# Graph-attention kernel: from the third head on, ScalarE copies the first of three value parts into packed rows of 132 bytes

## What is computed

```
feats = einsum('bnf,hfu->bhnu', X, W)
dense = e_self[..., :, None] + e_neigh[..., None, :]
dense = leaky_relu(dense, 0.2) + NEG_BIG * (1.0 - A)
att   = softmax(dense, axis=-1)
out   = einsum('bhij,bhju->bhiu', att, feats) + b
x     = layernorm(x + relu(out))
```

## Time and profile before

| what | value |
|---|---|
| median of 3 runs | 3373.38 us (3371.62 to 3376.89) |
| the profiled execution, its own time | 3371.02 us |
| its span, first to last instruction | 3369.2 us |
| PE busy | 3291.4 us, 98% |
| DVE busy | 2387.5 us, 71% |
| ACT busy | 1864.4 us, 55% |
| granted TensorE clock, mean | 0.995 of full |

### The profile page before, as it was taken

The page is one execution under the profiler, slowest core; times in us unless marked ns, Lnnn a source line. Parts: engine busy times, 40 slices in busy tenths (PEclk is TensorE's granted clock), DMA queues, the critical chain, the costliest instruction groups (busy, mean ns, idle before and its releaser), DMA issues.

```text
span 3369.2 us, 125185 instructions
## 1 busy us (share of the span) xinstructions
PE 3291.4 (98%) x57408; PEld 2804.7 (83%) x57408; DVE 2387.5 (71%) x4236; ACT 1864.4 (55%) x2456; POOL 283.6 (8%) x251
## 2 busy tenths in 40 slices
PE   5999999999999999999999999999999999999998
PEld 4978879798896978979789797887979879797896
DVE  4857758587685867858578585785858768586685
ACT  2746547365564645646466473654746547465563
POOL 0020100202001020010201002010020200202001
PEclk8999999999999999999999999999999999999999
DMA  6114141241412315132141421514124141231400
GB/s 189 62 51 135 45 125 54 69 123 40 132 60 83 102 34 141 65 85 94 39 139 54 101 78 43 142 47 123 56 64 127 41 132 60 73 112 34 126 29 25
DMA packets 233486, 280.95 MB, mean 83 GB/s; under 512 B 149888, under 2 KB 149888, under 8 KB 232960
## 3 DMA queue, kind: packets, MB, share of 16 engines
q1 hardware_dynamic: 232960, 272.95, 27.1%
HBM read 205.26 MB, written 34.08 MB: 71 GB/s over the span
## 4 chain that ended last, share of the span: by engine, by line
PE 85%; DVE 7%; DMA 5%; ACT 1%; issue 1%; SPq 0%; DVEq 0%; POOL 0%; ACTq 0%
PE six L856 72%; PE pair L856 10%; DVE mask L695 2%; DMA s_bc<-self_scores 2%; PE six L991 2%; DMA out_dram<-mask 1%; DMA self_scores<-sc_row 1%; PE pair L885 1%; DVE rest L603 1%; PE six L885 1%; DVE x_parts L599 1%; DVE feat L637 1%; ACT step L465 1%; DVE trl L632 0%; ACT trh L430 0%
## 5 line engine op out<-in xcount | busy, mean ns | idle before, releaser
L856 PE MATMUL six<-x_parts,mask 128*128 128x65 bf16 x16384 | 1547.0, 192 | 17.2 <-DVE mask L695 16.6
L856 PEld LDWEIGHTS six<-x_parts,mask 128*128 128x128 fp8e4 x16384 | 1536.2, 97 | 26.0 <-issue 16.0
L856 PE MATMUL six<-rest,mask 128*128 128x65 bf16 x16384 | 1547.1, 195 | 1.5 <-issue 1.2
L856 PE MATMUL six<-third,mask 128*128 128x65 bf16 x16384 | 1546.8, 192 | 0.8 <-issue 0.6
L856 PEld LDWEIGHTS six<-third,mask 128*128 128x128 fp8e4 x16384 | 1536.4, 98 | 1.3 <-issue 1.2
L856 PEld LDWEIGHTS six<-rest,mask 128*128 128x128 fp8e4 x16384 | 1531.0, 96 | 2.5 <-issue 1.8
L465 ACT ACTIVATE step<-s_bc,n_step 128x1024 uint16<-128x1024 f32 x1024 | 1089.4, 1137 | 372.4 <-DVE mask L695 342.9
L695 DVE TENSOR_TENSOR mask<-adj_t,step 128x1024 uint16<-128x1024 uint16 x1024 | 649.9, 685 | 55.9 <-ACT step L465 55.8
L856 PE MATMUL six<-adj_t,x_parts 128*128 128x512 fp8e4 x1536 | 388.4, 380 | 9.1 <-issue 4.9
L408 POOL TENSOR_TENSOR s_bc<-feat,rden 128x512 f32<-128x512 f32 x112 | 124.6, 1117 | 2811.3 <-DVE s_bc L738 2797.6
L856 PEld LDWEIGHTS six<-adj_t,x_parts 128*128 128x128 f16 x1536 | 146.3, 98 | 186.1 <-issue 15.9
(11 more groups left out here) (127 smaller groups left out, 4839.9 us busy)
## 6 DMA issues: line engine op xcount, KB each, us to landing
s_bc<-self_scores SPq DMA_DIRECT2D x128, 512.0 KB, 3.8
mask<-in_adj_dram SPq DMA_DIRECT2D x64, 512.0 KB, 4.0
xs<-in_x_dram SPq DMA_DIRECT2D x128, 256.0 KB, 3.6
adj_nat<-in_adj_dram SPq DMA_DIRECT2D x64, 512.0 KB, 3.5
out_dram<-mask SPq DMA_DIRECT2D x128, 256.0 KB, 3.3
adj_nat<-in_x_dram SPq DMA_DIRECT2D x64, 256.0 KB, 5.7
step<-in_x_dram SPq DMA_DIRECT2D x64, 256.0 KB, 3.8
xs<-in_L_gnn_W_dram SPq DMA_DIRECT2D x1, 2048.0 KB, 11.4
```

The lines of the kernel that those rows point to most:

```text
L856: return pe.matmul(o, l, r, start=start, stop=stop, skip_group_check=True)
```

## The change

A new tile `packed` holds the first part of a head as bf16, elements 2 bytes apart, in rows of 66 elements (132 bytes), with two buffers. For heads 2 to 7 of each batch ScalarE copies the upper halves of `val32` into it, once VectorE has written the float32 product (`val_f32`), and raises `val_packed`; TensorE waits for this at the start of the head and reads the first part from `packed`. Heads 0 and 1, the second part and the third part are as before. To make room, the small tile `wa32`, used once before the first batch, is laid over `key_w`.

```diff
+    PACKED_FROM = 2
...
+        packed = sb("packed", [P, 2, 2, T, U1 + 1], BF16)[:, :, :, :, 0:U1]
         val = [(upper_half(val32[i]), upper_half(rest32[i]), third[:, i]) for i in range(2)]
...
-        wa32 = sb("wa32", [P, KC, SC], F32)
+        wa32 = key_w[:, 0].rearrange("p t h -> p (t h)").rearrange("p (c n) -> p c n", c=KC)
...
+        val_packed = signal("val_packed", H - PACKED_FROM)
...
+                def pack_values(h):
+                    act.wait_ge(val_f32.sem, val_f32.at(b, h + 2))
+                    copy(packed[:, h % 2], val[h % 2][0]).then_inc(val_packed.sem, 1)
...
                 for g in range(H * T):
+                    if g % T == 0 and g // T >= PACKED_FROM:
+                        pack_values(g // T)
                     make_step(g)
...
+                    parts = val[h % 2] if h < PACKED_FROM else (packed[:, h % 2],) + val[h % 2][1:]
...
-                                         val[h % 2][part][:, kind, jt, :],
+                                         parts[part][:, kind, jt, :],
...
                     pe.wait_ge(val_p2.sem, val_p2.at(b, h + 2 if h else 1))
+                    if h >= PACKED_FROM:
+                        pe.wait_ge(val_packed.sem, val_packed.at(b, h - PACKED_FROM + 1))
```

## The result

The changed kernel takes 3359.24 us (median of 5 runs, 3357.29 to 3360.39), the kernel before in the same comparison 3374.02 (5 runs). The forecast was 3342: the direction was right, the size about twice too large (32 us against 15). The profiled execution took 3359.24 us, with a span of 3357.4.

A forecast was written before the change was run, and what follows sets the result against it. TensorE's matmul pace in the heads was taken as the bound. Saving 6 x 0.37 - 0.27 = 1.95 us in 15 batches and 2.2 in the last, 31.5 us, gave 3339.5 profiled, 3342 median; range 3333 to 3377.

The forecast's parts named there:

- What bounds the kernel: Value matmuls in the heads: TensorE hardly waits, so its pace counts, 93.6 ns a group of three, 31.2 ns a matmul.
- The price of the 4-byte step: First-part value matmuls on TensorE: reading elements 2 instead of 4 bytes apart saves 2.9 ns on each of 12288, 36 us.
- the rival of half the price: Packed first-part reads: only the 1.3 ns of the 512-column rows is saved, 16 us, giving 3357 us; chance 0.15.
- the whole 6.0 ns: Estimated excess of the long step in a group of three value matmuls, 35.2 ns against short steps of 29.2.
- the buffer that it was put down to: On TensorE, a supposed buffer between read and array, to explain why the long step isn't always behind the same part.
- ScalarE: 96 added copies, 1.1 us each, 106 us in all, fit in idle gaps before the heads' first steps; cost 0.
- What eats some of the gain: Heads 2 and 3, paced by ScalarE and VectorE too: TensorE would wait 0.27 us for a mask in head 3.
- the slack of 0.33: Head 3, sixth key tile: mask ready at 1164.57, used at about 1164.9, so TensorE can come 0.33 us earlier without waiting.
- The rows of 132 bytes: Rival in the packed tile: rows starting off 16-byte boundaries cost 2.9 ns on 9216 matmuls, 27 us slower, 3400; chance 0.09.
- Weights and output: What a group's three parts share, weight loads and 65 PSUM columns, sets the value matmuls' pace; nothing is shortened, chance 0.36.
- the rival of no gain: Value matmuls: weights or output shared by the three parts set the pace, ScalarE's copies are hidden, 3373 to 3375; chance 0.36.
- Lines of 16 bytes: SBUF reads: by the skill's rule two accesses to a line suffice, so packing 4-byte elements gains nothing; the forecast doubted it.

## Why the prediction was right or wrong

**What bounds the kernel**: right. PE's pace in the heads set the time, and each kernel's time followed its group.

**The price of the 4-byte step**: the term that failed. The sum took 2.9 ns for each of 12288 matmuls, 36 us; measured is 93.6 - 92.4 = 1.2 ns, 14.4 us in the heads and 15 in the times. The nearest row, 10.0 ns on 512 columns, 1.3 ns on 65, gave 16 us and stood in the text as the rival of half the price, 3357 us. The step that led away from it is the sentence that an excess which repeats every three matmuls needs something in which the three differ. It gave the two strided parts the whole 6.0 ns; with none strided 91.1 - 87.6 = 3.5 ns of them stay. The 14 groups that it was read from lie in one key tile. In the key tile before, the long step is behind another part, and with none strided a long step of 35 ns still comes once in five. The weak point that the text named, that the long step isn't always behind the same part, was the evidence against it; no run shows the buffer that it was put down to. Why a step is sometimes 6 ns longer stays open.

**ScalarE**: right. The copy takes 1.08 us (1.1 were said), leaves 1.04 us of the gap (0.9 were said), and alone costs nothing that can be told. The new wait on PE doesn't show.

**What eats some of the gain**: right as a mechanism, and too early. At 1.2 ns TensorE comes 0.15 x 1.63 = 0.24 us earlier at head 3's sixth key tile, within the slack of 0.33; the waits there are 0.8 us in the whole run, where the forecast had 0.27 in each batch. With 3.0 ns a group, in the kernel with both parts packed, the slack is gone and they are 4.6 us. The transposes that the text ahead of the forecast puts into heads 1, 2 and 3 stand in heads 1 and 2 on TensorE (key tiles 10, 13, 18, 21) and in heads 2 and 3 on the two others; the slack was read off the trace and doesn't depend on it.

**The rows of 132 bytes**: rightly left at a small chance; rows of 144 bytes are no faster. **Weights and output**, the rival of no gain: neither form tried was at fault, and the gain came.

**Lines of 16 bytes.** By the Trainium skill (Advanced Engine Details and Errata, Memory Cachelines) two accesses to a line of 16 bytes are enough for full speed, which would make elements 4 and 8 bytes apart free. At 4 bytes that was right to within 1.2 to 1.9 ns. At 8 bytes, two elements in 16 bytes, the matmul took 61.7 instead of 31.2 ns: there the measurement, on one constant tile, contradicts it.

## What to carry to other kernels

A moving operand with bf16 elements 4 bytes apart, such as the upper halves of float32 words, costs some 4 to 6% of a short matmul here (1.2 to 1.9 ns on 30.4), so that packing it pays only on an engine with idle time at the right place; elements 8 or 16 bytes apart, in the one tile tried, double or nearly quadruple the matmul. When a small excess is to be divided among causes, the nearest row that compares two cases directly is worth more than a pattern in the starts, and what remains without the suspect has to be asked for: one kernel that reads none strided would have shown it. A pattern in the starts is to be looked for in several key tiles before it is believed. As the bound engine becomes faster, the buffers' slack is read at its tightest place, not in its mean.

## What was not expected of the hardware

Moving operands of 64 and of 65 columns gave the same head, 11.98 us. With all three strided a group took 90 ns in one key tile and 100 ns in another, the same in nearly every late head and batch. And with no strided operand, whether the weights' bytes were adjacent or not, a group stayed at 91 ns, one step in five at 35 ns and the others at 29 or 30; what makes the long step is open.
